# Moving scans, statistics and output adds of the third layer between its gated rows

## The reference, cut to what matters

```
xn  = layernorm(x)
q, k, v = split(xn @ w_qkv); q, k = elu(q)+1, elu(k)+1
ksum_t  = decay*ksum_(t-1) + k_t          # scan over 512 tokens
kvsum_t = decay*kvsum_(t-1) + k_t*v_t
x1  = x + (q*kvsum / max(sum_d(q*ksum), 1e-6)) @ w_out
h   = silu(xn @ Wgate) * (xn @ Wup)       # 1024 hidden columns
x2  = x1 + rms_norm(h) @ Wproj
```

## Time and profile before

| | |
|---|---|
| time, median of 3 runs | 1003.14 us (1002.64 to 1003.33) |
| profiled execution | 1002.17 us, span 1000.4 us |
| TensorE busy | 938.4 us, 94% of the span |
| VectorE, ScalarE, GpSimd busy | 72%, 47%, 44% |
| third layer in the span | about 419 to 606 us |

### The profile page before, as it was taken

How to read it: one execution, slowest core, us unless ns; L and a number is a source line. 1 busy time by engine, 2 the same in 40 slices (tenths; PEclk the granted TensorE clock), 3 DMA queues, 4 the chain that set the end, 5 groups by cost and what they waited for, 6 DMA issues and landing times. The chain is left out here.

```text
span 1000.4 us, 12712 instructions
## 1 busy us (share of the span) xinstructions
PE 938.4 (94%) x4574; PEld 484.8 (48%) x4578; DVE 717.3 (72%) x1307; ACT 466.3 (47%) x771; POOL 437.3 (44%) x445
## 2 busy tenths in 40 slices
PE   9999889799999999779999999999999999999998
PEld 6777556233333433335565565524642564266325
DVE  4768676888888786567768756766777687759674
ACT  4333254266667676566546443712461345125411
POOL 3221476744444342234437341384058406830770
PEclk9999999799999999899999999999999999999999
DMA  9700064222212210120000001000000000000000
GB/s 312 258 17 16 16 173 144 74 66 65 61 37 64 65 33 2 69 82 17 1 16 1 16 1 46 0 1 1 22 1 1 1 22 0 1 1 22 1 1 22
DMA packets 28990, 43.68 MB, mean 44 GB/s; under 512 B 6560, under 2 KB 22128, under 8 KB 28528
## 3 DMA queue, kind: packets, MB, share of 16 engines
q1 hardware_dynamic: 28928, 42.87, 13.9%
HBM read 31.38 MB, written 11.27 MB: 43 GB/s over the span
## 5 line engine op out<-in xcount | busy, mean ns | idle before, releaser
L2239 POOL TENSOR_TENSOR l_scaled<-l_X,l_source 128x512 f32<-128x512 f32 x112 | 135.6, 1240 | 139.4 <-ACT l_X L2309 122.4
L1154 DVE TENSOR_REDUCE l_nmax<-banks 128x1 f32<-128x512 f32 (+1 forms) x165 | 147.8, 929 | 33.7 <-PE banks L1265 32.7
L1104 ACT ACTIVATE l1b_PT<-banks 128x512 f32<-128x512 f32 (+1 forms) x176 | 134.1, 793 | 65.8 <-PE banks L1278 65.4
L1265 PE MATMUL banks<-l_KQ 96*128 96x512 bf16 x240 | 81.3, 392 | 7.9 <-DVE l_nmax L1154 5.3
L1278 PE MATMUL banks<-l_KQ 99*128 99x512 bf16 x256 | 85.1, 385 | 2.3 <-ACT l1b_PT L1104 2.1
L2322 ACT ACTIVATE l_hhi<-l_h 128x512 f16<-128x512 f32 (+1 forms) x24 | 15.1, 630 | 129.4 <-DVE l_h L2434 129.4
L2658 PE MATMUL banks<-l_scaled,l_cbm 128*64 128x512 f32 x224 | 59.5, 613 | 10.7 <-POOL l_scaled L2239 10.6
L1292 PE MATMUL banks<-l1b_PT,l1b_V 128*32 128x512 f32 x512 | 68.2, 605 | 0.0
L2408 DVE TENSOR_TENSOR l_decayed<-banks,l_right_decay 128x512 f32<-128x512 f32 x56 | 38.4, 686 | 37.9 <-PE banks L2658 37.9
L2680 PE MATMUL banks<-l_decayed,w_place 64*128 64x512 f32 x224 | 63.2, 641 | 0.0
L1838 PE MATMUL banks<-l_xhi,l_ternary 128*128 128x512 f16 x128 | 48.6, 379 | 9.0 <-DVE l_h L1768 9.0
(11 more groups left out here) (350 smaller groups left out, 2072.0 us busy)
## 6 DMA issues: line engine op xcount, KB each, us to landing
l_split<-l1a_parts SPq DMA_DIRECT2D x16, 384.0 KB, 3.3
l_KQ<-l_split SPq DMA_DIRECT2D x48, 128.0 KB, 2.8
l_KQ<-l_split SPq DMA_DIRECT2D x16, 192.0 KB, 3.1
l_KQ<-l_split SPq DMA_DIRECT2D x48, 64.0 KB, 2.9
w_ternary<-l_tern_out SPq DMA_DIRECT2D x7, 384.0 KB, 2.3
l_raw<-in_w_gate_up SPq DMA_DIRECT2D x2, 1024.0 KB, 10.5
w_qkv<-in_w_qkv SPq DMA_DIRECT2D x2, 768.0 KB, 6.3
x<-in_x SPq DMA_DIRECT2D x3, 512.0 KB, 10.5
```

What stands on the lines that cost most here:

```text
L1104: nc.scalar.activation(PT[:, first:first + size, :], source, ACT.Exp, scale=SCALE).then_inc(p_ready, 1)
L1154: nc.vector.tensor_reduce(nmax[:, H % 2, first:first + size], source, axis=AX.X, op=ALU.max, negate=True).then_inc(smax_read, 1)
L1265: last = nc.tensor.matmul(ps[bank + m][:, :], KQ[pairs, QUERY, g, j, t * P:(t + 1) * P], KQ[pairs, KEY, g, j, :], start=True, stop=True)
L2239: nc.gpsimd.tensor_tensor(by_head(scaled[:, (2 * u + m) % 4, :]), by_head(X[:, T, :]), spread(source[:, level, T, :]), ALU.mult).then_inc( ...
```

## The change

In batch 0 the scans of channel half 0 move behind h(0) and those of half 1 behind h(1); in the other batches they stay where they were. `add_projected(b-1)` moves from the end of batch b-1 into rows 0 and 1 of batch b, two tiles each (for the last batch it stays at the end). The statistics move from row 0 to row 2, their second part to row 3, the shift to row 4, GpSimd's `invert` behind its second `add_square`, and ScalarE's `normalise` behind its row 5. TensorE's denominators wait only for qk and no longer for num; num has a semaphore of its own. In the last batch `sum_squares` goes ahead of `project_gated` and into bank 2.

```diff
-        DEN_AT, RT_AT, SPREAD_AT = 3, 5, 7
+        DEN_AT, RT_AT, SPREAD_AT = (3, 3, 3, 3), 5, 7
+        STATISTICS_AT = (2, 2, 2, 2)
+        def squares_bank(b):
+            return 6 if b + 1 < B else 2
...
             def weigh_queries(b):
-                nc.gpsimd.tensor_tensor(qk[:, :, :], feat[:, 0:CT, :], ksum[:, :, :], ALU.mult)
-                nc.gpsimd.tensor_tensor(num[:, :, :], feat[:, 0:CT, :], kvsum[:, :, :], ALU.mult).then_inc(qprod, 1)
+                nc.gpsimd.tensor_tensor(qk[:, :, :], feat[:, 0:CT, :], ksum[:, :, :], ALU.mult).then_inc(qprod, 1)
+                nc.gpsimd.tensor_tensor(num[:, :, :], feat[:, 0:CT, :], kvsum[:, :, :], ALU.mult).then_inc(num_ready, 1)
...
                 weigh_queries(b)
-                invert(b + 1)
                 for j in range(1, HT):
                     add_square(b, j)
+                    if j == STATISTICS_AT[b]:
+                        invert(b + 1)
...
-                    if j == 3:
+                    if j == STATISTICS_AT[b] + 3:
                         normalise(b + 1)
...
+            def variance():
+                own.settle()
+                dve.nop(nofuse=True)
+                for t in range(TT):
+                    last = nc.vector.bn_aggr(mv[:, t, :], stats[:, t, :])
+                own.link(last)
+                nc.vector.tensor_scalar(rstd[:, :], mv[:, :, 1], LN_EPS, None, ALU.add).then_inc(var_ready, 1)
...
                     if j:
                         rest_of_gated(b, j - 1)
-                    if j == 0:
-                        statistics(b + 1)
-                    if j == 1:
+                    if j < CT and b == 0:
+                        scan(b, (j,))
+                    elif j < CT:
+                        add_projected(b - 1, (2 * j, 2 * j + 1))
+                    if j == STATISTICS_AT[b]:
+                        statistics(b + 1, range(TT))
+                    if j == STATISTICS_AT[b] + 1:
+                        variance()
+                    if j == STATISTICS_AT[b] + 2:
                         shifts(b + 1)
...
                 if b + 1 < B:
                     features(b + 1)
-                    sum_up(b + 1)
+                    keys_times_values(b + 1)
+                    scan(b + 1, range(CT))
                 norm_gated(b)
-                add_projected(b)
+            add_projected(B - 1, range(TT))
...
             def sum_squares(b):
-                    pe.wait_ge(aout_added, b * 2 + 2)
+                    pe.wait_ge(h_ready, B * HT)
...
                     queries_keys_values(b + 1)
-                project_gated(b)
-                sum_squares(b)
+                    project_gated(b)
+                    sum_squares(b)
+                else:
+                    sum_squares(b)
+                    project_gated(b)
```

More of the change, by code:

```diff
@@ L1569, in layer2 @@
         qprod = sem("qprod")
+        num_ready = sem("num_ready")
         den_made = sem("den_made")
@@ L1701, in _, with statistics @@
             own = Own(dve, dve_own)
-            def statistics(b):
+            def statistics(b, tiles):
                 if b == B:
                     dve.wait_ge(x_done, TT)
-                norm_stats(k, dve, own, lambda t: k.x[:, b % B, t, :], stats, mv, rstd, var_ready)
+                for t in tiles:
+                    own.note(nc.vector.bn_stats(stats[:, t, :], k.x[:, b % B, t, :]))
+            def variance():
[5 more added lines that the diff above has]
+                nc.vector.tensor_scalar(rstd[:, :], mv[:, :, 1], LN_EPS, None, ALU.add).then_inc(var_ready, 1)
             def shifts(b):
@@ L1720, in features, with keys_times_values @@
                                                    ALU.add).then_inc(feat_ready, 1)
-            def sum_up(b):
+            def keys_times_values(b):
                 dve.wait_ge(feat_ready, b * 4 + 2)
@@ L1726, in sum_up, with scan @@
                     nc.vector.tensor_tensor(kv[:, c, :], feat[:, 2 + c, :], ps[V_BANK[c]][:, :], ALU.mult).then_inc(kv_ready, 1)
-                for c in range(CT):
+            def scan(b, channels):
+                for c in channels:
                     dve.wait_ge(kv_ready, b * CT + (c + 1))
@@ L1745, in norm_gated, with add_projected @@
                 dve.wait_ge(ss_made, b + 1)
-                nc.vector.tensor_scalar(inv[:, :], ps[6][:, 0:TT], 1.0 / HID, float(np.finfo(np.float32).eps),
+                nc.vector.tensor_scalar(inv[:, :], ps[squares_bank(b)][:, 0:TT], 1.0 / HID, float(np.finfo(np.float32).eps),
                                         ALU.mult, ALU.add).then_inc(ss_ready, 1)
-            def add_projected(b):
+            def add_projected(b, tiles):
                 dve.wait_ge(inv_ready, b + 1)
                 dve.wait_ge(aout_added, b * 2 + 2)
-                for t in range(TT):
+                for t in tiles:
                     dve.wait_ge(fout_made, b * 2 + (t // 2 + 1))
@@ L1759, in _ @@
             features(0)
-            sum_up(0)
+            keys_times_values(0)
             for b in range(B):
@@ L1783, in _ @@
                         nc.vector.reciprocal(rden[:, :, :], rden[:, :, :]).then_inc(rden_ready, 1)
+                dve.wait_ge(num_ready, b + 1)
                 for c in range(CT):
@@ L1897, in sum_squares @@
                 else:
-                    pe.wait_ge(aout_added, b * 2 + 2)
+                    pe.wait_ge(h_ready, B * HT)
                 for t in range(TT):
-                    last = nc.tensor.matmul(ps[6][:, t:t + 1], sqsum[:, t * P:(t + 1) * P], k.ones[:, 0:1], start=True, stop=True)
+                    last = nc.tensor.matmul(ps[squares_bank(b)][:, t:t + 1], sqsum[:, t * P:(t + 1) * P], k.ones[:, 0:1], start=True, stop=True)
                 last.then_inc(ss_made, 1)
@@ L1910, in _ @@
                     gates(b, j)
-                    if j == DEN_AT:
+                    if j == DEN_AT[b]:
                         denominators(b)
```

2 lines of the change are left out of this document (1 added, 1 removed).

## The result

| | before | after |
|---|---|---|
| time, median of 20 runs each | 1003.07 us (1000.13 to 1006.39) | 1008.37 us (1004.39 to 1011.89) |
| ratio of after to before, 95% interval | | 1.0048 [1.0036, 1.0060] |
| profiled execution, its span | 1002.17, 1000.4 us | 1009.35, 1007.6 us |
| granted clock of the profiled execution, mean | 0.986 | 0.979 |

The forecast was 1008.0, slower. The times of one kernel lie up to 7.5 us apart, far more than the other terms here, and they go with the granted clock: a straight line through the 20 runs of the changed kernel gives 0.74 us less for each 0.001 of mean clock. The means of the runs are 1008.20 us at 0.9804 (after) and 1003.80 at 0.9829 (35 runs of before beside the first experiments). So of 4.4 us between the means, 1.9 us go with the 0.0025 of clock, and about 2.5 us are left for work that comes later.

What follows compares the result with a forecast made beforehand. TensorE bounds it, 94% busy; in rows 0 to 5 the reciprocals set the turn. 0.5 + 0.5 + 0.75 + 0.8 - 0.3 = +2.25, with clock +4.85: 1007.0 profiled, 1008.0 us median; range 1001.0 to 1011.0.

Steps and rivals of the forecast that it cites:

- Batch 1: Rows 0 to 5: VectorE's reciprocals end at 497.16 against 496.66, so TensorE's turn of the denominators comes 0.5 us later.
- The hold of the shift: Row 4: VectorE's shift waits for GpSimd's add_square(3), about 1.2 us instead of 0.16; bounds nothing and 1.77.
- Rival B: Row 4: the shift isn't held, turns come 0.4 to 0.5 us earlier, -2.1 in all, 1001.0 us; chance 0.20.
- Batch 2: Same steps as Batch 1: the turn of the denominators comes 0.5 us later.
- Batch 3: No line 2048 ahead of the reciprocals, h(4) gains only 0.46, shift held 1.2: turn 0.75 us later.
- Batch 0: Scans between rows, late qk, shift held by add_square(3): reciprocals 0.65 to 1.0 us later, 0.8 taken.
- TensorE ... is still 1.4 early: Batch 0: TensorE idles 3.6 us before the denominators, yet stays 1.4 us ahead of its earlier timeline.
- The moved normalise: ScalarE between rows 5 and 6: normalise ends near 498.1 in batch 1, before silu(6) at 498.7, so costs nothing.
- The end: Last batch: x is done near 603.45 instead of 605.55, but keep_going still follows; 0.3 us gained, bounds 0.3 and 1.0.
- The clock: Behind the longer pauses before the turns TensorE's granted clock falls twice, 1.3 us each: 2.6 us; bounds 0 and 6.8.
- that returns 1.7 of what was won: Batch 1: rest(0) starts inside GpSimd's num at 486.16, is held to 488.49, and gives back 1.7 us.

Runs made afterwards that it cites:

- the first experiments: Runs 1 to 4, made on one chip beside runs of the kernel before, which had a mean of 1003.80 us at clock 0.9829.
- Run 1: The changed kernel with VectorE's shift behind the reciprocals instead of ahead of them: median 1004.72 us, ratio to before 1.0014.
- Run 5: The changed kernel with the shift behind the reciprocals and batch 0's scans back ahead of h(0): median 1001.94 us, ratio to before 0.9979.
- run 4: The changed kernel with batch 0's scans back in one piece ahead of h(0): median 1008.59 us, ratio to before 1.0033.
- run 2: The changed kernel with four unread products on TensorE ahead of the wait for the reciprocals: median 1006.28 us, ratio to before 1.0041.
- run 6: The changed kernel with two unread products on TensorE ahead of the wait for the reciprocals: median 1005.72 us, ratio to before 1.0027.
- run 7: The changed kernel with GpSimd's num behind the third add_square instead of behind qk: median 1009.88 us, ratio to before 1.0076.
- run 3: The kernel before with only the last batch's sum_squares moved ahead of project_gated, into bank 2: median 1001.36 us, ratio to before 0.9982.
- Run 9: The kernel before with only ScalarE's normalise moved from behind row 3 to behind row 5: median 1006.44 us, ratio to before 1.0039.
- Run 11: The kernel before with the last batch's sum_squares ahead of project_gated and without the three unread products at the layer's end: median 1002.60 us, ratio to before 1.0003.
- run 10: Run 5 with rest(0) moved behind h(2) and the statistics in row 1 instead of row 2: median 997.01 us, ratio to before 0.9946.

## Why the prediction was right, point by point

The total was met within 0.4 us, and that is partly luck: batch 0 cost more than its term, batches 1 to 3, the end and the clock less, and the errors cancel.

**Batch 1: right, to 0.1 us.** h(0) was forecast at 483.85 and stands at 487.85, so 4.0 is to be taken off. Then rest(0) starts at 486.18 (forecast 486.16) and ends at 488.51 (488.49), h(4) starts at 493.50 (493.57), the shift at 494.71 (494.78), the turn at 497.1 (497.2). Against before the turn lies later by 0.36 and not 0.5, which is this last 0.1. The hold of the shift was taken as 1.2, from a square of 1.27, and the shift took 1.23. Run 1 shows that it decides, 1.14 us.

**What the hold rests on.** The small operation stood until the square was through, in batches 1, 2 and 3, and not in batch 0, where none ran. The Trainium skill (GPSIMD Engine Reference, Key points) names VectorE instructions in a two-port mode or with two SBUF inputs as those in contention with GpSimd. For the ones with two SBUF inputs this trace agrees: 1.23 and 2.33 us beside a square and num, instead of 0.16 and 0.68. They aren't the only ones. Line 106, which the earlier trace rows show at 0.56 beside num, has one input; after the change the same operation (line 1722) takes 0.82 beside a square in batch 0, and 0.17 in batch 1 with GpSimd idle. Rival B needed the shift to slip through in its place, and no run has that. Run 5 takes it out of the way instead, with the scans back as well: the turns come 0.38 a batch sooner than before, where B said 0.5, and the time is 1001.94, where B said 1001.0.

**Batch 2: right with the clock.** +1.68 is 0.36 and a fall of 1.3. **Batch 3: right,** +0.60 against 0.75.

**Batch 0: the size off, and another mechanism.** The forecast was a shift held by add_square(3), 0.8 later. VectorE, GpSimd there:

```profile
445.69 2.47 DVE L1754 TENSOR_TENSOR l_hlo<-l_h,l_hhi 128x512 f16<-128x512 f32 x1
...
453.84 0.69 DVE L1786 TENSOR_TENSOR l_h<-l_act_gate,banks 128x512 f32<-128x512 f32 x1 [1.77 <-PE banks L1864]
...
456.15 0.15 DVE L1726 SCALAR_TENSOR_TENSOR l_shift<-l_mv,l_rstd 128x4 f32<-128x4 f32 x1
```

```profile
445.27 2.34 POOL L1633 TENSOR_TENSOR l_qk<-l_feat,l_ksum 128x1024 f32<-128x1024 f32 x1 [17.81 <-DVE l_kvsum L1749]
```

qk came late (445.27) and held rest(1), as forecast, and TensorE lost 3.5 us before the denominators (3.37 and the 0.16; 3.6 forecast). But then the clock fell, h(4) had to wait 1.77 for its gates, and the shift met no square (0.15). The step that failed is "TensorE ... is still 1.4 early": at the 1.2 GHz level it was not early but last. In this execution it made 1.77 instead of 0.8; run 4 puts 1.46 of it on the scans. A fall that begins behind the denominators, between 447 and 452 us, lies in all five profiles with the scans between the rows (the change, runs 1, 2, 6 and 7). In the seven other runs, with the scans ahead of h(0), it begins at 441 to 447. There it can cost nothing, where TensorE has to wait for h(1) next: run 3 has this fall and before hasn't, and turn 0 comes at 34.13 and 34.11 us.

**The moved normalise, "free": right for the change, not in itself.** Run 9 shows 0.24 a batch when the turn follows the gates of row 5 closely. In runs 1 and 5, behind the late shift, it eats part of what the shift gives.

**The end: in its bounds, mis-sized.** 0.64 instead of 0.3 (bounds 0.3 and 1.0). The two adds stand behind project_gated, and the products followed, as forecast:

```profile
611.91 2.74 PE L113 MATMUL banks<-w_qkv,ident 128*128 128x512 f32 x6
```

```profile
614.91 1.28 ACT L2283 ACT_TABLE_LOAD   x1 [17.56 <-PEq L1519]
```

They end at 614.65 and layer four begins 0.26 behind (TensorE 0.30); I had added 0.5, the distance from x before, to the end of the products. Run 11 shows that the mechanism, the meeting waits for the products, was right.

**The clock: right in the mean, not understood.** Two falls of 1.3 were forecast; 1.9 us is what the means of the runs show, and a fall costs 1.3 to 1.7 in a period (44.94 against 43.63 in the change; 44.56 with one in run 1, 42.89 without in run 5), more at the layer's end, as shown above. What makes it fall is only partly shown. Products in the pause before the turn go with a higher mean clock (0.9824 in runs 2 and 6). But the pause was shortened in run 1 without that (0.9800), and the wait of 3.37 in batch 0 was taken away in run 4 without that (0.9808). With both away it is 0.9827 (run 5), and with half of what was left of the pause away 0.9846 (run 10). Against before in their own groups that is 0.0029 and 0.0021 less, then 0.0006 less and 0.0005 more. That either alone keeps it low fits these numbers, but at 12 runs each they can't prove it, and run 9, 0.0027 below before without either of the two waits, speaks against their being the whole of it.

**What the prediction missed** is where the gain was. It took the held rest(0) as given ("that returns 1.7 of what was won") and weighed only whether the shift would be held too. Moved behind h(2), with the statistics in its place, it gave 0.82 us a batch, more than the shift's 0.74.

## What to carry to other kernels

Moving work on an engine towards "earlier" is worth only what the last waiter on the same engine gets; here the reciprocals, with two held operations ahead of them. Before placing a VectorE operation with two SBUF inputs, however small, look for a GpSimd operation that runs then. Beside it put what these traces show unheld: operations that read a bank, bn_stats, the reciprocal (0.55). Behind it put the ones with two SBUF inputs. That an operation has one input is no safe sign, as line 106 shows. Where a kernel's runs lie 0.7% apart with the clock, read the size of a step from a repeated stretch without a fall, and the verdict from many runs; the two can differ, as in run 4.

## What the runs showed that I had not expected

- The hold doesn't go by the size of the held operation. The shift, 128x4, took 1.23 us and ended when the square beside it did (498.71 + 1.23 = 499.94, against 498.57 and half of 2.76 = 499.95). The rest, 128x512, took 2.33 and ended 0.55 behind num (492.51, against 489.60 + 2.36 = 491.96), about its own length. Both stood until GpSimd was through and then ran.
- A fall of the clock changes what meets what: behind turn 3 of the change two falls cost 4.52 us, with 3.34 us of clock.
- Squares queued on GpSimd run without a gap between them, but VectorE's held operation gets in where one ends: the shift is through at 499.94, between two squares that fill 498.57 to 501.33.
- The same pause of 2.74 to 2.75 us was followed by a fall in one batch and by none in the next.
- Taking away the three products at the layer's end, which cost 1.41 us there, won nothing in the time; the mean clock was lower (0.9817 against 0.9838).
